# Expert layer: gate and up computed with the weights as the stationary operand, straight code, eight buffers

## What is computed

```python
sorted_xs = x_flat[xs_indices, :]                      # tokens gathered expert by expert
gate_out = ragged_dot(sorted_xs, w_gate, group_sizes)  # (rows, 256) @ (256, 2 * 256) of the row's expert
gate_out = gate_out.reshape(rows, 2, H)
activation = gelu(gate_out[:, 0, :]) * gate_out[:, 1, :]
expert_outputs = ragged_dot(activation, linear, group_sizes)   # (rows, 256) @ (256, 256)
...
out = einsum('blkd,blk->bld', out, combine_weights)
```

## Time and profile before

| | before |
|---|---|
| median of 3 runs | 931.17 us (931.12 to 932.04) |
| the profiled execution | 941.12 us, its span 939.4 us |
| TensorE busy | 812.5 us (86%) |
| VectorE busy | 562.1 us (60%) |
| ScalarE busy | 483.2 us (51%) |
| GpSimd busy | 390.0 us (42%) |
| expert stage, first to last work on TensorE | about 640 to 872 us |

### The profile page before, as it was taken

How to read it: one execution, slowest core, us unless ns; L and a number is a source line. 1 busy time by engine, 2 the same in 40 slices (tenths; PEclk the granted TensorE clock), 3 DMA queues, 4 the chain that set the end, 5 groups by cost and what they waited for, 6 DMA issues and landing times. The chain is left out here.

```text
span 939.4 us, 17505 instructions
## 1 busy us (share of the span) xinstructions
PE 812.5 (86%) x5618; PEld 426.3 (45%) x5619; DVE 562.1 (60%) x1560; ACT 483.2 (51%) x1011; POOL 390.0 (42%) x456
## 2 busy tenths in 40 slices
PE   5989601799999999999999999856999999999598
PEld 2555400134444444444444444313555656555497
DVE  4767364988888888888888888301222222222177
ACT  2333300067777777777777777852333333333374
POOL 3545340033223233322323332323666666665398
PEclk9999855589999999999999999996999999999799
DMA  4999899295555666555566600009222222222485
GB/s 157 221 263 269 213 107 121 34 253 74 62 61 57 82 81 81 67 62 61 59 82 81 81 3 3 2 6 321 86 84 84 84 84 84 84 85 78 129 245 182
DMA packets 115004, 100.32 MB, mean 107 GB/s; under 512 B 58172, under 2 KB 95676, under 8 KB 114876
## 3 DMA queue, kind: packets, MB, share of 16 engines
q1 hardware_dynamic: 105976, 80.50, 46.9%
q0 software_dynamic: 8960, 18.95, 6.4%
HBM read 63.89 MB, written 35.00 MB: 105 GB/s over the span
## 5 line engine op out<-in xcount | busy, mean ns | idle before, releaser
L784 ACT ACTIVATE probs<-spsum 128x512 f32<-128x512 f32 x576 | 312.1, 604 | 169.6 <-PE spsum L835 163.8
L742 DVE CUSTOM_DVE_ANT_0 junk<-mpsum,mask 128x128 bf16<-128x128 f32 (+7 forms) x512 | 360.0, 754 | 58.5 <-issue 51.7
L824 PE MATMUL mpsum<-ks,qs 102*128 102x512 bf16 (+3 forms) x768 | 183.5, 343 | 45.9 <-DVE cpsum L731 26.3
L722 POOL TENSOR_SCALAR_AFFINE_SELECT probs<-probs 128x512 f32<-128x512 f32 x128 | 78.8, 634 | 340.8 <-ACT probs L784 340.8
L835 PE MATMUL spsum<-qs,ks 105*128 105x512 bf16 (+3 forms) x768 | 199.2, 329 | 10.6 <-ACT probs L784 8.3
L855 PE MATMUL cpsum<-probs,vs 128*17 128x256 f32 (+2 forms) x2560 | 152.7, 360 | 1.5 <-POOL probs L722 0.8
L1037 PE MATMUL gu<-w_gu,xTs 128*128 x288 | 139.2, 607 | 1.7 <-ACT xTs L981 1.7
L1016 DVE COPY hT<-hp 128x256 f32<-128x256 f32 x72 | 30.6, 425 | 167.8 <-PE hp L1044 100.6
L824 PEld LDWEIGHTS mpsum<-ks,qs 102*128 102x128 bf16 x768 | 69.8, 100 | 122.5 <-DVE maxima L742 39.8
L835 PEld LDWEIGHTS spsum<-qs,ks 105*128 105x128 bf16 x768 | 67.1, 97 | 102.9 <-ACT probs L784 52.9
L956 POOL DMA_INDIRECT expert_rows<-y,places x72 | 70.7, 983 | 72.2 <-ACT y L990 42.2
(11 more groups left out here) (124 smaller groups left out, 698.5 us busy)
## 6 DMA issues: line engine op xcount, KB each, us to landing
qk_parts<-parts SPq DMA_DIRECT2D x32, 384.0 KB, 4.4
qs<-qk_parts SPq DMA_DIRECT2D x96, 128.0 KB
ks<-qk_parts SPq DMA_DIRECT2D x96, 128.0 KB
yk<-expert_rows SPq DMA_DIRECT2D x32, 256.0 KB, 3.1
v_rows<-vt SPq DMA_DIRECT2D x32, 136.0 KB, 4.5
vs<-v_rows SPq DMA_DIRECT2D x16, 272.0 KB, 12.0
x_in<-in_x SPq DMA_DIRECT2D x8, 512.0 KB, 6.3
xn_rows<-xn SPq DMA_DIRECT2D x8, 512.0 KB, 5.8
```

What stands on the lines that cost most here:

```text
L722: pool.affine_select(out=part, in_=part, compare_op=ALU.is_ge, fill=0.0, base=0, pattern=[[0, 4], [1, P]], channel_multiplier=-1).then_inc ...
L742: last = dve.tensor_tensor_reduce(junk[:, slot, c:c + w], mpsum[:, slot, c:c + w], keep["mask"][:, S - w:S], 1.0, 3 * NEG, ALU.add, ALU.ma ...
L784: act.activation(probs[:, u % PRING, h], spsum[:, (4 * u + h) % SRING], ACT.Exp, scale=SCALE).then_inc(exp_done, 1)
L824: last = pe.matmul(mpsum[:, slot, at + c:at + e], qs[hq][0:R_MAX, h, qt * P:(qt + 1) * P], ks[hq][0:R_MAX, h, c:e], start=True, stop=True)
```

## The change

- `gate_up` is turned round. The weights are the stationary operand and the rows stream: for each of 4 blocks c of 128 output columns and each half dh, `w_now[:, dh, 128c:128(c+1)]` is loaded and 128 columns of `xT` stream past it. As a float32 matmul is two instructions, there are 16 a tile. `gu` now has the hidden units as partitions and the rows as columns, which is what `down` wants.
- So VectorE's product goes straight to `hT`. `hidden_T`, `hp`, `hid` and the copy L1016 go.
- VectorE copies the weights of tile s + 2's expert (1024 columns a partition) from `w_gu` to `w_now` (two buffers) after the product of tile s, with the expert's number in a register of VectorE. `gate_up` waits for it (`w_ready`).
- No loops: TensorE, ScalarE and VectorE have all 72 tiles written out. The order on TensorE becomes gate_up(s), rows_T(s + 2), down(s - 1); it reads one expert number a turn. The order on ScalarE is gelu(s), xT_copy(s + 2), store(s - 1).
- `down(s)` waits for `y_ready` of tile s - 2. RR is 8: `rows` and `y` have eight buffers.

```diff
--- before.py
+++ after.py
@@ -895,7 +895,7 @@
 def experts(nc, ins, scratch, keep, last_weights):
 
 
-    RR = 4
+    RR = 8
     AHEAD = 6
     with ExitStack() as ctx:
         sb = lambda name, shape, dt=F32: ctx.enter_context(nc.sbuf_tensor(name, shape, dt))
@@ -906,12 +906,11 @@
         places = sb("places", [P, NST, 2], I32)
         xT = sb("xTs", [P, 2, DH, P])
         gate = sb("gate", [P, 2, HID])
-        hid = sb("hid", [P, 2, HID])
+        w_now = sb("w_now", [P, 2, DH, 2 * HID])
         hT = sb("hT", [P, 2, DH, P])
         y = sb("y", [P, RR, D])
         tp = ctx.enter_context(nc.psum_tensor("tp", [P, 2, CH], F32))
         gu = ctx.enter_context(nc.psum_tensor("gu", [P, 2, CH], F32))
-        hp = ctx.enter_context(nc.psum_tensor("hp", [P, 2, CH], F32))
         yp = ctx.enter_context(nc.psum_tensor("yp", [P, 2, CH], F32))
         w_in = sem("w_in")
         places_in = sem("places_in")
@@ -919,16 +918,9 @@
         y_out = [sem(f"y_out{i}") for i in range(RR)]
         y_free, passed = sem("y_free"), sem("passed4")
         tp_ready, xT_ready = sem("tps_ready"), sem("xTs_ready")
-        gu_ready, gate_ready, hid_ready = sem("gu_ready"), sem("gate_ready"), sem("hid_ready")
-        hp_ready, hT_ready = sem("hp_ready"), sem("hT_ready")
+        gu_ready, gate_ready, hT_ready, w_ready = sem("gu_ready"), sem("gate_ready"), sem("hT_ready"), sem("w_now_ready")
         yp_ready, y_ready = sem("yp_ready"), sem("y_ready")
         block = ctx.enter_context(nc.Block())
-
-        def tiles(eng, body):
-
-            with eng.Fori(0, NST // 2) as i:
-                for par in range(2):
-                    body(2 * i + par, par, i)
 
         @block.sync
         def _(sp):
@@ -976,111 +968,89 @@
         @block.scalar
         def _(act):
 
-            def xT_copy(s, par):
+            def xT_copy(s):
                 act.wait_ge(tp_ready, s + 1)
-                act.activation(xT[:, par].rearrange("p a t -> p (a t)"), tp[:, par, 0:D], ACT.Copy).then_inc(xT_ready, 1)
-
-            def gelu(s, par):
+                act.activation(xT[:, s % 2].rearrange("p a t -> p (a t)"), tp[:, s % 2, 0:D], ACT.Copy).then_inc(xT_ready, 1)
+
+            def gelu(s):
                 act.wait_ge(gu_ready, s + 1)
-                act.activation(gate[:, par], gu[:, par, 0:HID], ACT.Gelu_apprx_tanh).then_inc(gate_ready, 1)
-
-            def store(s, m):
+                act.activation(gate[:, s % 2], gu[:, s % 2, 0:HID], ACT.Gelu_apprx_tanh).then_inc(gate_ready, 1)
+
+            def store(s):
                 act.wait_ge(yp_ready, s + 1)
                 act.wait_ge(y_free, s + 1)
-                act.activation(y[:, m], yp[:, m % 2, 0:D], ACT.Copy).then_inc(y_ready, 1)
-
-            xT_copy(0, 0)
-            gelu(0, 0)
-            xT_copy(1, 1)
-            gelu(1, 1)
-            xT_copy(2, 0)
-            with act.Fori(0, NST // RR - 1) as i:
-                for j in range(RR):
-                    s = RR * i + 2 + j
-                    gelu(s, j % 2)
-                    xT_copy(s + 1, 1 - j % 2)
-                    store(s - 2, j)
-            for s in range(NST - 2, NST + 2):
-                if s < NST:
-                    gelu(s, s % 2)
-                if s + 1 < NST:
-                    xT_copy(s + 1, (s + 1) % 2)
-                store(s - 2, (s - 2) % RR)
+                act.activation(y[:, s % RR], yp[:, s % 2, 0:D], ACT.Copy).then_inc(y_ready, 1)
+
+            xT_copy(0)
+            xT_copy(1)
+            for s in range(NST):
+                gelu(s)
+                if s + 2 < NST:
+                    xT_copy(s + 2)
+                if s >= 1:
+                    store(s - 1)
+            store(NST - 1)
 
         @block.vector
         def _(dve):
-            def body(s, par, i):
+            def weights(s):
+
+                e = dve.value_load(keep["tile_expert"][0:1, s:s + 1], min_val=0, max_val=NE - 1)
+                dve.tensor_copy(w_now[:, s % 2].rearrange("p a c -> p (a c)"), w_gu[:, ds(e * DH, DH)].rearrange("p a c -> p (a c)")).then_inc(w_ready, 1)
+
+            dve.wait_ge(keep["w_gu_in"], 16 * NE)
+            weights(0)
+            weights(1)
+            for s in range(NST):
                 dve.wait_ge(gate_ready, s + 1)
-                dve.tensor_tensor(hid[:, par], gu[:, par, HID:2 * HID], gate[:, par], ALU.mult).then_inc(hid_ready, 1)
-                dve.wait_ge(hp_ready, s + 1)
-                dve.tensor_copy(hT[:, par].rearrange("p a t -> p (a t)"), hp[:, par, 0:HID]).then_inc(hT_ready, 1)
-
-            tiles(dve, body)
+                dve.tensor_tensor(hT[:, s % 2].rearrange("p a t -> p (a t)"), gu[:, s % 2, HID:2 * HID], gate[:, s % 2], ALU.mult).then_inc(hT_ready, 1)
+                if s + 2 < NST:
+                    weights(s + 2)
 
         @block.tensor
         def _(pe):
-            pe.wait_ge(keep["w_gu_in"], 16 * NE)
-
-            def rows_T(s, m, i):
-
-                pe.wait_ge(rows_in[m], 16 * (i + 1))
+            def rows_T(s):
+
+                pe.wait_ge(rows_in[s % RR], 16 * (s // RR + 1))
                 for dh in range(DH):
-                    last = pe.transpose(tp[:, m % 2, dh * P:(dh + 1) * P], rows[:, m, dh * P:(dh + 1) * P], keep["ident"][:, :])
+                    last = pe.transpose(tp[:, s % 2, dh * P:(dh + 1) * P], rows[:, s % RR, dh * P:(dh + 1) * P], keep["ident"][:, :])
                 last.then_inc(tp_ready, 1)
 
             def expert_of(s):
-                return pe.value_load(keep["tile_expert"][0:1, ds(s, 1)], min_val=0, max_val=NE - 1)
-
-            def gate_up(s, par, e):
+                return pe.value_load(keep["tile_expert"][0:1, s:s + 1], min_val=0, max_val=NE - 1)
+
+            def gate_up(s):
+
                 pe.wait_ge(xT_ready, s + 1)
+                pe.wait_ge(w_ready, s + 1)
+                for c in range(2 * HID // P):
+                    for dh in range(DH):
+                        last = pe.matmul(gu[:, s % 2, P * c:P * (c + 1)], w_now[:, s % 2, dh, P * c:P * (c + 1)],
+                                         xT[:, s % 2, dh], start=dh == 0, stop=dh == DH - 1)
+                last.then_inc(gu_ready, 1)
+
+            def down(s, e):
+                pe.wait_ge(hT_ready, s + 1)
+                if s >= 2:
+                    pe.wait_ge(y_ready, s - 1)
                 for dh in range(DH):
-                    last = pe.matmul(gu[:, par], xT[:, par, dh], w_gu[:, ds(e * DH + dh, 1)].rearrange("p a c -> p (a c)"),
-                                     start=dh == 0, stop=dh == DH - 1)
-                last.then_inc(gu_ready, 1)
-
-            def hidden_T(s, par):
-                pe.wait_ge(hid_ready, s + 1)
-                for dh in range(DH):
-                    last = pe.transpose(hp[:, par, dh * P:(dh + 1) * P], hid[:, par, dh * P:(dh + 1) * P], keep["ident"][:, :])
-                last.then_inc(hp_ready, 1)
-
-            def down(s, par, e):
-                pe.wait_ge(hT_ready, s + 1)
-                for dh in range(DH):
-                    last = pe.matmul(yp[:, par, 0:D], hT[:, par, dh], w_down[:, ds(e * DH + dh, 1)].rearrange("p a c -> p (a c)"),
+                    last = pe.matmul(yp[:, s % 2, 0:D], hT[:, s % 2, dh], w_down[:, ds(e * DH + dh, 1)].rearrange("p a c -> p (a c)"),
                                      start=dh == 0, stop=dh == DH - 1)
                 last.then_inc(yp_ready, 1)
 
-
-
-            rows_T(0, 0, 0)
-            gate_up(0, 0, expert_of(0))
-            rows_T(1, 1, 0)
-            gate_up(1, 1, expert_of(1))
-            hidden_T(0, 0)
-            rows_T(2, 2, 0)
-            gate_up(2, 0, expert_of(2))
-            pe.wait_ge(w_in, 16 * NE)
-
-            def turn(s, j, i):
-
-                coming, going = expert_of(s + 1), expert_of(s - 2)
-                hidden_T(s - 1, (j + 1) % 2)
-                rows_T(s + 1, (j + 1) % RR, i + (j + 1) // RR)
-                down(s - 2, j % 2, going)
-                gate_up(s + 1, (j + 1) % 2, coming)
-
-            with pe.Fori(0, NST // RR - 1) as i:
-                for j in range(2, 2 + RR):
-                    turn(RR * i + j, j, i)
-            turn(NST - 2, 2, NST // RR - 1)
-            hidden_T(NST - 2, 0)
-            down(NST - 3, 1, expert_of(NST - 3))
-            hidden_T(NST - 1, 1)
-            down(NST - 2, 0, expert_of(NST - 2))
-            last_expert = expert_of(NST - 1)
-            pe.wait_ge(y_ready, NST - 2)
-            down(NST - 1, 1, last_expert)
+            rows_T(0)
+            rows_T(1)
+            going = expert_of(0)
+            for s in range(NST):
+                gate_up(s)
+                if s + 2 < NST:
+                    rows_T(s + 2)
+                if s == 1:
+                    pe.wait_ge(w_in, 16 * NE)
+                if s >= 1:
+                    down(s - 1, going)
+                    going = expert_of(s)
+            down(NST - 1, going)
 
 
 def combine(nc, ins, scratch, keep, last_weights, out):
```

## The result

Measured first: 916.68 us (916.19 to 917.79) against 931.61 us (931.12 to 932.3) before, ratio 0.9833 with an interval of 0.9816 to 0.985. The same kernel, run again later, gave 0.9807 [0.9795, 0.982], and on yet another chip 1.0065 [1.0041, 1.0088]: faster by 1.7 to 1.9% twice, slower by 0.65% once. The two results need two explanations.

The account below looks back on a forecast made before the run. TensorE's queue was taken to bound the expert stage, 3.02 us a turn becoming 2.83. Removing 22.1 us, less 0.15 and 72 x 0.02, with some tenths back at the end, gave 21 us off 931.17: 910 us, range 906 to 943.

Parts of the forecast that it names:

- the hidden transpositions and the jumps: Taken off TensorE's path: 72 x 0.22 = 15.8 us of transpositions and 17 loop jumps x 0.37 = 6.3 us, together 22.1.
- Gate and up: On TensorE, 16 load and matmul pairs at 0.109 us make 1.74 us a tile, 0.02 more than before; new turn 2.83.
- Rival (b): TensorE's weight loads don't hide at 128 columns: 11 us per 0.01 us a pair, about 1004 at 0.193; chance 0.12 beyond 0.128.
- Copy and slack: VectorE's weight copy takes 0.70 us (about 1.2 if slow); TensorE wants it with slack of 1.4 us or more, so no cost.
- GpSimd: Two indirect DMAs a turn have a floor of 2.54 us; a turn of 2.83 leaves 0.29, the next thing to be late.
- Rival (a): VectorE's copy and GpSimd's DMAs exclude each other: 919.6 to 940.9 us; chances 0.26 faster, 0.05 within 0.2%, 0.10 slower.
- p = 2.81: GpSimd's time per turn in us, from which its being held up by VectorE's copies would set the kernel's time.
- Start: TensorE at stage start: tile 1's gather taken to land at 642.4, gate and up 2 to start 0.15 us later than before.
- The total: Expert stage ends 21 us earlier (871.6 to 850.7): profiled 941.12 becomes 920.1, and 931.17 without the profiler becomes 910.2.
- rival (c): The loop jump's 0.37 us stays in some form on TensorE, as longer straight code must be fetched: 916 us; chance 0.05.
- ScalarE keeps its three activations, 1.15 us a turn: ScalarE's work per turn in the expert stage was taken as unchanged at 1.15 us.
- The slack of hT: TensorE's down(s) waits for hT(s): 3.04 us are available for the 1.22 us that gelu and multiply need.

Follow-up runs that it names:

- a_straight: The kernel before with the three loops of the expert stage (TensorE, ScalarE, VectorE) written out, nothing else changed: 930.28 us, ratio 0.9919 to the kernel before.
- e_double: The changed kernel with a second VectorE copy of the same 1024 columns to a spare buffer behind each weight copy: 918.05 us, ratio 0.9808 to the kernel before.
- g_after: The changed kernel, unchanged, run again beside the kernel before on another chip: 918.62 us, ratio 0.9807.
- d_before: The kernel before, unchanged, profiled once more: 935.65 us.
- l_again: The changed kernel, unchanged, run once more on yet another chip: 951.04 us against 943.64 for the kernel before, ratio 1.0065.

## Why the prediction was right or wrong

On the chips of the quicker pace the sum holds, as to its mechanism. Point by point:

- **Removed: the hidden transpositions and the jumps.** Right. No turn has the 0.22, and a_straight puts the jumps at 7.6 us [6.4, 8.8] against 6.3.
- **Gate and up.** The term was 1.74 us, the measured one 1.78. I took 0.109 a pair, the lower end, "the row nearest to it", from transpositions; ordinary pairs cost 0.111, most likely because the load leads. With the turn at 2.867 in place of 2.83 this is 69 x 0.037 = 2.6 us of lost gain. Rival (b) had the mechanism right (no room under the load) at a small size; its slower case began at 0.128.
- **Copy and slack.** 0.70 us was said, 0.69 measured. Gate and up never waited for it in the steady state of after or e_double. Right.
- **GpSimd.** Its two DMAs take 0.96 + 1.15 us and two gaps of 0.30, 2.71 of the 2.87, so the room is 0.16 us and not 0.29 (in g_after, with 1.06 and 1.10, it is 0.11). Rival (a) had the mechanism right in part: copy and DMA do exclude each other, over parts of the DMA. Wrong was the price of 0.40 or 0.70 a turn; it is 0.17 to 0.22, and its bound of p = 2.81 was nearly reached (2.54 + 0.22 = 2.76). The forecast put this term at nothing, and that the time did not show it is by so small a margin partly luck.
- **Start.** Tile 1 landed 2.15 after tile 0, against the 1.95 I took. I worked out gate and up 2 at 11.35 us after TensorE's first work. It was 9.44, since the clock was up earlier; in d_before it was 8.99. So 0.45 us is lost there by profiles of the same pace, and one wait for rows (651.76) costs 1.0.
- **The total.** I expected 21 us, against a profile of before whose stage took 231.2 us. Against 228.9 it is 16.9. Of the missing 4.1 us, 2.3 are the clock at the start of that one profile of before; 1.8 are in the kernel after, whose stage I had at 850.7 - 640.45 = 210.2: 2.6 for the pairs and 1.0 for the wait for rows, less 1.9 for the earlier start. The measured 916.68 lies 6.7 above the forecast, in the range, at the edge of the forecast's own (906 to 917). It is also within a microsecond of the 916 of rival (c), by chance: no turn of after has the jump's time. The first runs gained 14.9 us, 2 less than the profiles; whether that is their chip or the scatter of four runs stays open.

What the prediction did not have is the case that l_again shows. It gave 0.22 to slower, by GpSimd or by the weight loads; the kernel is slower by 0.65% on one chip through a third way, ScalarE's gelu coming late. The step that failed there is the one which says "ScalarE keeps its three activations, 1.15 us a turn": it counts ScalarE's work and takes for granted that its instructions are there on time. The slack of hT was worked out (3.04 us for 1.22, so 1.8), and it is what the late gelus overrun: 4.2 late less 1.8 is 2.4, and 2.1 was waited.

What makes ScalarE late is not settled. After writes out 72 tiles for three engines. The queues of the page of l_again (packets, MB, share) have 50 and 36 packets of instructions, as after has, where before has 37 and 31, so the written-out code comes with more such packets:

```profile
q8 instruction: 50, 0.82, 0.4%
q14 instruction: 36, 0.29, 0.1%
```

From 656 to 872 us l_again has 20 of these packets, and the late gelus come at some 24 places, about every 10 us; they don't fall on the packets one by one. The Trainium skill, "Runtime: NRT & Kernel Launch", section Instruction fetch mechanics, holds that streaming straight code is mostly hidden. The quiet runs agree with it (a_straight gained all of the jumps); l_again neither confirms nor refutes it: rival (c) in a wider sense, straight code that comes too late, is not excluded for the chips of the slower pace. Why the chips differ stays open too.

## What to carry to other kernels

When the stationary and the streamed operand change places, price the new form by its weight loads: at 128 columns a float32 pair costs about what its load costs, 0.111 us, and the product is ready turned for the next one. A loop's back edge on the engine that bounds the kernel is worth counting (0.37 us here). And before a gain of one or two per cent is believed, run both kernels on several chips: first look whether a stage that was not touched has the same pace in both profiles, then whether an engine with nothing to wait for starts late.

## What the runs showed of the hardware

- Pairs of ordinary float32 load and matmul run at 0.110 to 0.111 us, whether 64 or 128 columns stream; the recorded load of 192 ns overlaps.
- A jump back of the loop costs TensorE about 0.37 us, and written out the same code costs nothing on the chip where it was tried.
- A float32 copy of 1024 columns on VectorE (0.69 us) and an indirect DMA of GpSimd (0.96 to 0.98 us) exclude each other over parts of the DMA. One that starts inside the copy ends 0.85 us after it; one into which the copy starts 0.45 to 0.48 us after its beginning ends 0.12 us after the copy (g_after, 1.27 us). A copy that starts 0.54 to 0.78 us in is itself held (up to 0.94 us). The same copy on ScalarE (1.06 us) leaves the scatter at 0.98.
- The same attention code idles ScalarE 160 us in some profiles and 169 in others, and takes 427.5 or 435 us, by chip.
- In the profiles of that slower pace, ScalarE started gelus up to 4.2 us after their input stood, about half of them, once the turn was 2.87 us, while VectorE and GpSimd were on time. After two of twelve waits of TensorE in l_again, of 2.03 and 2.09 us, its granted clock was 0.50 for 3.4 us, which added 1.6 to 1.7 us each.
